# A gated recurrence by chunks, and a last mixture of experts whose results go through indirect transfers

## The reference

```
x_conv = _causal_depthwise_conv(x, conv_weight, conv_bias)
r_t = jax.nn.sigmoid(x_conv @ Wr_w.T + Wr_b)
i_t = jax.nn.sigmoid(x_conv @ Wi_w.T + Wi_b)
a_t = jnp.power(a_base[None, None, :], 8.0 * r_t)
b_t = jnp.sqrt(jnp.clip(1.0 - a_t * a_t, 1e-06, None)) * (i_t * x_conv)
h = _parallel_scan(a_t, b_t)
return _rmsnorm(h @ out_w.T, norm_w)
```

```
idx = jnp.argsort(-score, axis=0)[:cap].T
xe = xf[idx]
hact = jax.nn.silu(gate) * upv
ye = jnp.einsum('ecj,eoj->eco', hact, w_down)
out = jnp.zeros((T, C), xf.dtype).at[idx.reshape(-1)].add((w[..., None] * ye).reshape(-1, C))
```

## Time and profile before

| | us |
|---|---|
| median of 3 runs | 3968.68 (3968.6 to 3971.08) |
| the profiled execution, its own time | 3984.97 |
| its span in the profile | 3982.6 |
| mean granted clock of TensorE, share of full | 0.934 |
| `normalise` and `gated_recurrence` | 455 to 556 |
| `mixture_3` | 3750 to 3982.6 |
| cross attentions, the largest three stages | most of the rest |

### The profile page before, as it was taken

One profiled execution on the slowest core, in us unless ns is written; L12 is line 12 of the kernel. 1 busy time (PEld: TensorE's weight loads), 2 busy tenths in 40 slices (PEclk: granted clock), 3 DMA queues, 4 the chain that ended last, 5 costly groups with the idle time before them and its releaser, 6 DMA issues. The chain is left out here.

```text
span 3982.6 us, 111770 instructions
## 1 busy us (share of the span) xinstructions
PE 3484.1 (87%) x47616; PEld 2402.3 (60%) x47616; DVE 2460.2 (62%) x4562; ACT 2087.3 (52%) x2854; POOL 1587.6 (40%) x1859
## 2 busy tenths in 40 slices
PE   7976549999999698879999999798898999999739
PEld 5654227777777444647777777343445777777537
DVE  4522477877777354458877776233567877777554
ACT  3334437666666222137666666334445766666412
POOL 1100027667675000036766664000336676766210
PEclk9998769999999798889999999799999999999859
DMA  4063116565655153026556564110015656655412
GB/s 157 2 257 121 45 42 152 140 155 145 155 146 120 29 120 89 3 63 154 148 144 156 140 155 96 45 58 22 31 23 133 154 145 153 148 143 147 135 37 69
DMA packets 201821, 435.87 MB, mean 109 GB/s; under 512 B 87634, under 2 KB 96936, under 8 KB 201160
## 3 DMA queue, kind: packets, MB, share of 16 engines
q1 hardware_dynamic: 199048, 427.02, 40.7%
q0 software_dynamic: 864, 1.48, 0.1%
q10 hardware_dynamic: 1440, 0.52, 0.1%
HBM read 183.46 MB, written 2.42 MB: 47 GB/s over the span
## 5 line engine op out<-in xcount | busy, mean ns | idle before, releaser
L1480 DVE TENSOR_REDUCE x_bank_top<-ps 112x1 f32<-112x500 f32 x2304 | 1419.2, 672 | 463.8 <-PE ps L1199 457.0
L1337 ACT ACTIVATE x_probs_t<-ps 128x1344 f32<-128x1344 f32 x768 | 990.7, 1291 | 204.7 <-PE ps L1218 200.2
L1218 PEld LDWEIGHTS ps<-x_queries,x_keys 128*128 128x128 bf16 x9216 | 486.9, 98 | 315.3 <-issue 146.4
L1199 PE MATMUL ps<-x_keys,x_queries 96*112 96x500 bf16 x2304 | 634.1, 381 | 22.7 <-DMA x_queries<-x_query_part 15.9
L1218 PE MATMUL ps<-x_queries,x_keys 128*128 128x112 bf16 x9216 | 582.2, 213 | 24.5 <-ACT x_probs_t L1337 20.2
L1231 PE MATMUL ps<-x_probs_t,x_values 128*32 128x112 f32 x18432 | 487.0, 262 | 4.8 <-ACT x_probs_t L1337 4.8
L1231 PEld LDWEIGHTS ps<-x_probs_t,x_values 128*32 128x32 f32 x18432 | 440.5, 111 | 69.0 <-issue 63.5
L1413 POOL TENSOR_TENSOR x_key_part<-x_key_whole,x_nothing 128x500 bf16<-128x500 f32 x270 | 337.4, 1250 | 253.3 <-ACT x_key_whole L1322 253.3
L1417 POOL TENSOR_TENSOR x_key_part<-x_key_left,x_nothing 128x500 bf16<-128x500 f32 x270 | 340.7, 1262 | 21.2
L1199 PEld LDWEIGHTS ps<-x_keys,x_queries 96*112 96x112 bf16 x2304 | 259.2, 131 | 126.2 <-DVE x_bank_top L1480 32.8
L1187 PE MATMUL ps<-x_wv,x_ctx_t 128*128 128x128 f32 (+1 forms) x2304 | 330.1, 287 | 0.4 <-issue 0.4
(11 more groups left out here) (507 smaller groups left out, 4387.4 us busy)
## 6 DMA issues: line engine op xcount, KB each, us to landing
x_keys<-x_key_part SPq DMA_DIRECT2D x1152, 192.0 KB, 3.7
x_ctx_t<-in_ctx_t SPq DMA_DIRECT2D x96, 750.0 KB, 5.9
cm_ctx_n<-in_ctx_n SPq DMA_DIRECT2D x32, 768.0 KB, 6.0
cm_ctx_t<-in_ctx_t SPq DMA_DIRECT2D x32, 750.0 KB, 8.2
x_queries<-x_query_part SPq DMA_DIRECT2D x558, 28.0 KB, 2.7
e_share<-m_weight_rows SPq DMA_DIRECT2D x32, 448.0 KB, 5.6
m_w<-in_L_ffn_experts SPq DMA_DIRECT2D x16, 768.0 KB, 6.2
e_share<-m_weight_rows SPq DMA_DIRECT2D x8, 896.0 KB, 5.3
```

The costliest lines, as they stand in the source:

```text
L1199: nc.tensor.matmul(ps[0:RW, n, 0:KB], queries[i // 2 % 2][0:TALL, p, i % 2, :], keys[i % 2][0:TALL, p, KB * n:KB * n + KB], start=True, st ...
L1218: mm = nc.tensor.matmul(ps[:, turned_bank(i, p) + c // VC, RW * (c % VC):RW * (c % VC) + RW], keys[i % 2][:, p, KT * c:KT * c + KT], queri ...
L1337: nc.scalar.activation(probs_t[PROBS[p]].rearrange("k (n c) r -> k n (c r)", c=VC), ps[:, turned_bank(i, p):turned_bank(i, p) + VR, 0:VC * ...
L1480: nc.vector.tensor_reduce(bank_top[0:RW, p, n:n + 1], ps[0:RW, n, 0:KB], AX_X, ALU.max).then_inc(topped, 1)
```

## The change

In `gated_recurrence` the normalisation is drawn into the stage, every step goes by chunks of 448 real columns, POOL takes four kinds of pass (decay, clip, cap, feed), the doubled exponent comes from ACT, and the last square root and reciprocal become a logarithm and an exponential on ACT. In `mixture_3` the near-zero test is an absolute value on ACT and one comparison on DVE; the rounds of the search alternate between two buffers; the first group of gathered tiles has 2 instead of 4; `up` runs one pair ahead of `down` on doubled buffers; masks, bf16 parts and the L2069 matmuls are gone. In their place POOL writes each weighted tile by an indirect transfer into a table in DRAM that SP has filled with zeros, and at the end SP reads the table back and PE adds the two rows of every token by matmuls with an identity. In five waits of the router PE runs matmuls whose results nobody reads (`stay_busy`).

```diff
         @block.sync
-            sp.dma_start(token_names[:], chip.dram["m3_tokens"].to_broadcast([P, T])).then_inc(s["tokens_landed"], 16)
+            answers_of = answers.rearrange("(c t q k) d -> c q t k d", c=CH, t=TC, k=2)
+            sp.wait_ge(s["zeroed"], 1)
+            for c in range(CH):
+                sp.dma_start(answers_of[c].rearrange("q t k d -> q t (k d)"), zeros[:]).then_inc(s["emptied"], 16)
...
+            sp.wait_ge(s["scattered"], 16 * TILES)
+            for c in range(CH):
+                sp.dma_start(back[c][:], answers_of[c]).then_inc(answers_landed[c], 16)
...
         @block.tensor
+            def stay_busy(n):
+                for _ in range(n):
+                    nc.tensor.matmul(ps[:, RESULT + 1, 0:CT], chip.mean[:], chunk[0], start=True, stop=True)
...
             mm.then_inc(s["routed_turned"], 1)
+            stay_busy(16)
             pe.wait_ge(s["tops_ready"], 1)
...
-                for j in finished(n - 2):
-                    scatter(j)
                 if n < PAIRS:
                     down(n)
+            for c in range(CH):
+                pe.wait_ge(answers_landed[c], 16)
+                for t in range(TC):
+                    for k in range(2):
+                        mm = nc.tensor.matmul(ps[:, c, PAIR * t:PAIR * t + PAIR], back[c][:, t, k, :], chip.ident[0:PAIR, 0:PAIR], start=(k == 0), stop=(k == 1))
+                mm.then_inc(s["summed"], 1)
...
         @block.scalar
+                norm.wait_scaled(act, c)
+                nc.scalar.activation(few[c].rearrange("p (b s) -> p b s", s=S), chunk[c], ACT.Abs).then_inc(s["absolute"], 1)
...
         @block.gpsimd
+            pool.wait_ge(s["emptied"], 16 * CH)
+            for j in range(TILES):
+                r = slice(0, lines_in(j))
+                pool.wait_ge(s["weighted"], j + 1)
+                nc.gpsimd.indirect_dma_start(answers, bass.IndirectOffsetOnAxis(ap=rows_u[r, j:j + 1], axis=0), answer[r, j, :], None,
+                                             bounds_check=2 * T - 1, oob_is_err=False).then_inc(s["scattered"], 16)
```

The recurrence's new streams on POOL and ACT, and its chain on DVE:

```diff
+        @block.gpsimd
+            for c in range(CH):
+                pool.wait_ge(s["r_kept"], c + 1)
+                nc.gpsimd.tensor_scalar(decay[c], r_gate[c], rate[:, 0:1], float(np.log(np.float32(1e-7))), ALU.mult, ALU.max).then_inc(s["decay_ready"], 1)
+            for c in range(CH):
+                pool.wait_ge(s["summed"], c + 1)
+                nc.gpsimd.tensor_scalar(cumulated[c], cumulated[c], -80.0, None, ALU.max).then_inc(s["clipped"], 1)
+                pool.wait_ge(s["doubled"], c + 1)
+                nc.gpsimd.tensor_scalar(root[c], root[c], 1.0, -1.0, ALU.min, ALU.mult).then_inc(s["capped"], 1)
+            for c in range(CH):
+                pool.wait_ge(s["i_kept"], c + 1)
+                nc.gpsimd.tensor_tensor(i_gate[c], conv[c], i_gate[c], ALU.mult).then_inc(s["fed"], 1)
         @block.scalar
+            for c in range(CH):
+                act.wait_ge(s["clipped"], c + 1)
+                nc.scalar.activation(shrink[c], cumulated[c], ACT.Exp, scale=-1.0).then_inc(s["shrunk"], 1)
+                nc.scalar.activation(grow[c], cumulated[c], ACT.Exp).then_inc(s["grown"], 1)
+            for c in range(CH):
+                act.wait_ge(s["capped"], c + 1)
+                nc.scalar.activation(root[c], root[c], ACT.Sqrt, bias=1.0).then_inc(s["root_ready"], 1)
         @block.vector
+            def recur(c):
+                dve.wait_ge(s["root_ready"], c + 1)
+                dve.wait_ge(s["fed"], c + 1)
+                nc.vector.scalar_tensor_tensor(root[c], root[c], 1e-3, i_gate[c], ALU.max, ALU.mult).then_inc(s["scaled_in"], 1)
...
+                nc.vector.tensor_tensor(root[c], root[c], shrink[c], ALU.mult).then_inc(s["inputs_ready"], 1)
...
+                nc.vector.tensor_tensor_scan(state[c], alive[:], root[c], 0.0, ALU.mult, ALU.add).then_inc(s["recurred"], 1)
...
+                nc.vector.tensor_tensor(state[c], state[c], grow[c], ALU.mult).then_inc(s["h_ready"], 1)
```

More of the change, by code:

```diff
@@ new lines, in _, with power_of @@
+            pe.wait_ge(s["out_landed"], 2 * 16)
+            def power_of(c):
+                pe.wait_ge(s["squared"], c + 1)
+                nc.tensor.matmul(ps[:, 4 + c, 0:CT], chip.mean[:], power[c], start=True, stop=True).then_inc(s["power_done"], 1)
+            for c in range(CH):
+                pe.wait_ge(s["h_ready"], c + 1)
+                nc.tensor.matmul(ps[:, c, 0:CT], wo[:], state[c], start=True, stop=True).then_inc(s["out_done"], 1)
+                if c:
+                    power_of(c - 1)
@@ L872, in _ @@
[L872 to L880, removed]
@@ L881, in _ @@
-            step(nc.scalar.activation(i_gate[:], work[:], ACT.Exp, scale=-1.0))
-            nc.scalar.activation(work[:], work[:], ACT.Exp).then_inc(root_ready, 1)
+                norm.square(act, c)
+            act.wait_ge(s["rate_landed"], 16)
+            nc.scalar.activation(rate[:], log_a[:], ACT.Exp, scale=-1.0).then_inc(s["rate_part"], 1)
+            nc.scalar.preload_act_table_set("natural_log")
+            act.wait_ge(s["rate_part"], 1)
+            nc.scalar.activation(rate[:], rate[:], ACT.Ln, bias=1.0).then_inc(s["rate_part"], 1)
@@ L883, in _ @@
+            for c in range(CH):
+                norm.log(act, c)
             for c in range(CH):
[L884 to L887, removed]
+                norm.inverse(act, c)
+            act.wait_ge(s["gates_landed"], 4 * 16)
             for c in range(CH):
-                act.wait_ge(power_done, c + 1)
@@ new lines, in keep_gathered, with gate @@
+                nc.scalar.copy(tokens_of[:, P * tiles[0]:P * tiles[-1] + P], ps[:, TURN, 0:P * len(tiles)]).then_inc(s["gathered_kept"], 1)
+            def gate(n):
+                act.wait_ge(s["up_done"], n + 1)
+                nc.scalar.activation(silu[n % 2].rearrange("p a k -> p (a k)"), ps[:, GATE + n % 2, 0:BLOCKS * CAP], ACT.Silu).then_inc(s["gate_kept"], 1)
+            for g in range(groups_for(0)):
+                keep_gathered(g)
+            gate(0)
+            for g in range(groups_for(0), groups_for(1)):
+                keep_gathered(g)
@@ L2148, in _ @@
+            for n in range(PAIRS):
+                if n + 1 < PAIRS:
+                    gate(n + 1)
+                    for g in range(groups_for(n + 1), groups_for(n + 2)):
+                        keep_gathered(g)
+                act.wait_ge(s["down_done"], n + 1)
+                nc.scalar.copy(results[:, 2 * CAP * n:2 * CAP * n + 2 * CAP], ps[:, DOWN, 0:2 * CAP]).then_inc(s["down_kept"], 1)
         @block.gpsimd
@@ L2321, in _ @@
+            slot_step = Step(dve, s["slot_chain"])
+            hide(0)
+            for g in range(groups_for(1)):
+                weigh_slots(g)
+            for n in range(PAIRS + 1):
+                if n + 1 < PAIRS:
+                    hide(n + 1)
+                    for g in range(groups_for(n + 1), groups_for(n + 2)):
+                        weigh_slots(g)
+                for j in finished(n - 1):
+                    weigh(j)
             for c in range(CH):
```

385 lines of the change are left out of this document (184 added, 201 removed).

## The result

The changed kernel takes 3932.34 us (median of four, 3914.59 to 3935.49) against 3969.88 for the kernel before (3968.6 to 3979.41). The ratio is 0.9887, with an interval of 0.9862 to 0.9913, so 37.5 us are gained. The forecast was 3951 with a range of 3925 to 3966. The time lies inside it and the sign is right, but only half of the gain was forecast (17.8).

A forecast was written before the change was run, and what follows sets the result against it. The prediction took chain length to bound the recurrence and PE to end last in the experts' loop; -30.8 (recurrence), +0.9 (last stage through the loop) and +12.1 (end) gave -17.8, so 3951 us, range 3925 to 3966.

The forecast's parts named there:

- The recurrence: Stage `gated_recurrence`: chunked steps with POOL sharing the passes end it at 525.2 against 556.0, -30.8 us.
- the lower bound: Recurrence: only -25 us if POOL and DVE passes hinder each other, with three scans and four feeds paid in full.
- The router: Last stage before the experts: near-zero test -3.4 us, search -1, unread matmuls -1, first group of two tiles -2.5.
- unread matmuls: Router waits: matmuls with unread results give a higher clock for short PE steps, -1 us, bounds -3 to +2.
- Rival C: Router: the unread matmuls overrun their waits at clock 0.50, +11 us in all, giving 3962; chance .04.
- The end: From last down to the finish: indirect writes, read back, PE additions and store take 26.1 us, +12.1.
- My forecast is a loop that stays at 0.50: Experts' loop on PE: slower clock gives back the 2.27 us a pair saved; +0.9 for the last stage so far.
- The midway case: Experts' loop: the clock rises only partway through, spreading the time over 3900 to 3937; chance .03.
- A: The forecast itself: experts' loop at clock 0.50, total about 3937 to 3965; chance .75.
- B: Experts' loop at clock 1.00: 59.4 us in place of 112.5, total 3895; chance .13.
- Rival D: Experts' loop: pair 1's wait for weight loads recurs, five pairs of sixteen, total 3977 or more; chance .05.

The follow-up runs named there:

- the narrow kernel: Twelve unread matmuls of 70 columns added ahead of the fourth up of the changed kernel; second run 3945.18 us, ratio 0.9926.
- the first three experiments: Recurrence edits alone on the kernel before, 0.9931; changed kernel without unread matmuls, 0.9881; changed kernel with four 448-column unread matmuls before the fourth up, 0.9859.

## Why the prediction fell short

That the time lies in the range is partly luck. The loop was forecast 8.8 us longer and came out 15.9 shorter, and the low end of the range was meant for a clock that rises in the last few pairs. The prediction's own closing sentence names a clock other than 0.50 in the loop as the sign of being wrong, and for the last seven ups it stood at 1.00.

**The recurrence** was right: 29.0 gained, 30.8 forecast, and POOL is what it hangs on, at 500.95 against 500.5; with its passes on DVE it is 10.6 us shorter. The mechanism of the lower bound was real in a smaller size. POOL's last decay took 2.63 and its first clip 2.17 (1.33 alone), both beside scans on DVE, and the first chunk's chain 2.4 us longer than alone. The Trainium skill, "SBUF — State Buffer", section "Who interferes with whom", says that a DVE pass with two inputs in SBUF and a GpSimd pass that reads SBUF contend. The runs agree that they hinder each other (1.46 against 0.62), though only some of the passes paid. Nor was it true that no row of before has POOL beside such a DVE pass. There was one of 16 columns beside POOL's L2160, which runs from 3772.60 for 1.13 us:

```profile
3772.90 0.86 DVE L2190 TENSOR_TENSOR m_sums<-m_halves 128x16 f32<-128x16 f32 x1
```

It ends with POOL's pass, and takes 0.19 in the change, where POOL is idle.

**The router** was forecast well, and each term came a little larger: near-zero test -5.0 for -3.4, since a comparison takes 0.38 and not 0.57; the search 20.47 to 19.05, -1.4 for -1; first group -2.9 for -2.5; unread matmuls -0.45 for -1, part of it within the -2.9. Rival C, an overrun, did not come here: all five kept inside their waits. In three other profiles, at the lower clock, the group of three filled its wait to the end (4.1 to 4.2 us), so the margin is small.

**The end** costs +9.2 for +12.1. The read lands in 4.3 us rather than 6.0, the store takes 3.1 rather than 5.1, and PE's additions take 9.8 for 8.9.

**The step that failed** is the sentence "My forecast is a loop that stays at 0.50". Its parts held: the clock falls at the entry, a run of 70-column matmuls without a gap didn't raise it, and a cold pair takes 7.12 where 7.5 was put. It took the matmuls of L2069 for what raises the clock and concluded that without them nothing would. But the loop has other instructions: turnings of four tiles of 128 columns, after every third or fourth pair. Behind one of these the clock rose, and then held without L2069. In before one of them (3882.09) stands right ahead of the first L2069, whose twelve took 2.92 us and the next twelve 2.43; so the clock rose 1.0 us into them and 2.0 behind the start of the turning, and the row can't tell the two apart. The change, the kernel without unread matmuls, the one with groups (twice) and the two with passes on DVE all have the rise within 2 us of the start of such a turning. But others passed without one, among them all four in the narrow kernel, and no run added or removed a turning. That they are the cause is therefore argued and not shown. The midway case, given a chance of .03, was the one that came: eight ups at 0.50. The profiles of kernels with the change's own loop show nearly the whole span of cases: raised at the entry (last stage 183.2), behind the fifth up (197.8), behind the ninth (215.8 and 215.5); and in the one with only narrow matmuls added it was never raised (244.5, of which 5.3 are those). So something near A and something near B were both possible courses of one loop. The chances were put on one or the other, and the right forecast was a spread between them.

The gain from removing L2069 (2.27 us a pair) is real only at full clock, 5.99 to 3.71 a pair; at 0.50 a pair takes 7.12, and the loop that was never raised is longer than that of before (124.3 less 5.3 for the narrow ones, against 112.6). Rival B's price is confirmed: 67 us from the first up to the end of the last down (6.3 to the second up, 59.4 and 1.3), against 64.3 measured. Rival D did not come: the creep of some 5 us stood once in after, as in before.

The Trainium skill, "TensorE: Matmul & The Clock Gate", Part 1, has activity release the throttle. In these runs PE was busy for 123.17 of 124.30 us at 0.50, so as a rule on busy time it does not hold here. The same part ("HAM oscillation") advises against idle gaps, and here the trace agrees: a stretch of 2.43 us without work took the clock from 1.00 to 0.50 in the kernel with gathers in groups, and filling the entry's gaps kept it at 1.00. The gaps that mattered here, under a microsecond at the entry, are shorter than those it speaks of.

**Open:** what the creep in pair 2 is. It came in five profiles of nine with the gathers all at once (before, after, and the first three experiments), and in none of three with groups. But the experiments ran on three chips. On the first all three with the gathers at once had it and the one with groups had not, and on the two others no profile at the usual speed had it, whatever the gathers. So the groups are only tested against it in one profile, and the chip is a rival. Which turning raises the clock in an execution, if it is the turning, was not settled either.

## What to carry to other kernels

Before taking wide matmuls out of a loop of narrow ones, look at the granted clock in stretches where only the narrow ones run. Here the narrow loop kept 1.00 for 64 us when it was entered at 1.00, but did not come back to it reliably once it had fallen, and then every pair cost 7.12 us in place of 3.71. Filler work belongs in the last gaps ahead of the loop (here five more matmuls, in gaps under a microsecond, went with a median of 3891 in place of 3932, and the thirty-six in the long waits before them gave 0.45). And a pass goes to an idle engine only if it takes about as long there: here POOL took 1.33 for what DVE did in 0.32 (1.27 for four), while DVE waited for it.

## What was not expected of the hardware

- Twenty-four matmul instructions of 70 columns (5.33 us of unbroken work) left the clock at 0.50 in the place where eight of 448 columns (5.22 us) had raised it to 1.00.
- A loop of the same code took 64.6 us at a mean clock of 0.97 in one profile and 96.7 at 0.66 in another; with 24 narrow instructions added it took 124.3 at 0.50.
- A DVE pass of 448 columns with two inputs took 1.46 us beside a POOL pass, and 0.62 without.
- In one execution in this study PE's instructions took 1.6 to 2.4 times as long as usual in the whole program (the largest groups), 8142.53 us in all, while the profile shows a granted clock of 1.00 throughout.
